# Second-layer gathers that wait for counted sums; the counts made once, in the first stage

## The reference

```python
# layer 2 (GIN): edge_attr is 100000 x 256
msg = relu(x[src] + edge_attr)
aggr = segment_sum(msg, dst)
h = relu((x + aggr) @ W1 + b1) @ W2 + b2
out = layernorm(x + relu(h), gamma, beta)
# layer 3 (GCN)
out = segment_sum((x @ W)[src] * edge_weight, dst) + b
```

## Time and profile before

| | |
|---|---|
| median of 3 runs | 6718.57 us (6707.67 to 6720.85) |
| profiled execution | 6709.51 us, span 6707.9 us |
| TensorE clock granted, mean over the span | 0.782 |
| stages in the trace (about) | first stage to 135 us; second layer's edges 1631 to 2834; third layer's edges 3038 to 4533 |

### The profile page before, as it was taken

The page is one execution under the profiler, slowest core; times in us unless marked ns, Lnnn a source line. Parts: engine busy times, 40 slices in busy tenths (PEclk is TensorE's granted clock), DMA queues, the critical chain, the costliest instruction groups (busy, mean ns, idle before and its releaser), DMA issues. The chain is left out here.

```text
span 6707.9 us, 101753 instructions
## 1 busy us (share of the span) xinstructions
PE 4589.8 (68%) x18270; PEld 3405.7 (51%) x18271; DVE 4578.5 (68%) x11385; ACT 2738.4 (41%) x8093; POOL 4024.3 (60%) x3678
## 2 busy tenths in 40 slices
PE   5466666650566666787777777766577777777799
PEld 4234434430333333476666666655455555555688
DVE  4466666676454454587777777766489989888554
ACT  0233333335333333252111111113298899888543
POOL 2666666633666666426888888881377777777110
PEclk8666676675767777897777777778788898988899
DMA  7344444424555655426888888886466666666110
GB/s 239 104 107 107 111 108 109 107 78 159 171 176 176 183 177 177 123 67 119 136 135 136 136 135 137 135 116 225 147 182 190 182 187 187 187 183 180 37 32 28
DMA packets 698838, 940.86 MB, mean 140 GB/s; under 512 B 99488, under 2 KB 555552, under 8 KB 698721
## 3 DMA queue, kind: packets, MB, share of 16 engines
q0 software_dynamic: 270624, 580.57, 37.7%
q1 hardware_dynamic: 408658, 339.19, 17.8%
q10 hardware_dynamic: 19440, 19.79, 0.9%
HBM read 756.06 MB, written 183.11 MB: 140 GB/s over the span
## 5 line engine op out<-in xcount | busy, mean ns | idle before, releaser
L1864 POOL DMA_INDIRECT gcn<-c_update,c_target x784 | 1227.4, 1566 | 265.0 <-issue 203.8
L696 POOL DMA_INDIRECT e_rows<-hrow,e_idx x832 | 820.7, 986 | 465.0 <-issue 234.8
L2240 POOL DMA_INDIRECT s_rows<-kv,s_idx x832 | 800.4, 962 | 397.1 <-issue 214.3
L1249 POOL DMA_INDIRECT g_rows<-x,g_idx x784 | 772.5, 985 | 388.1 <-issue 228.6
L759 PE MATMUL psum<-e_rows,e_onehot 128*128 128x265 f32 x1664 | 667.1, 556 | 292.5 <-DVE acc L853 124.3
L1368 PE MATMUL psum<-g_rows,g_onehot 128*128 x1664 | 606.0, 527 | 217.5 <-ACT g_rows L1272 169.9
L2354 PE MATMUL psum<-queries_sums,s_spread 128*128 x1664 | 523.7, 469 | 261.8 <-issue 153.4
L1330 DVE TENSOR_TENSOR acc<-acc,psum 128x1024 f32 x208 | 253.7, 1220 | 592.2 <-DMA n_bias<-in_l_bias 338.8
L759 PEld LDWEIGHTS psum<-e_rows,e_onehot 128*128 128x128 f32 x1664 | 396.9, 264 | 501.5 <-DVE acc L853 217.5
L1368 PEld LDWEIGHTS psum<-g_rows,g_onehot 128*128 128x128 f32 x1664 | 418.8, 264 | 421.9 <-issue 346.8
L1841 ACT COPY acc<-psum 128x512 f32<-128x512 f32 x208 | 121.9, 586 | 1157.2 <-PE psum L1795 618.9
(11 more groups left out here) (381 smaller groups left out, 9433.8 us busy)
## 6 DMA issues: line engine op xcount, KB each, us to landing
g_attr<-in_edge_attr SPq DMA_DIRECT2D x196, 512.0 KB
acc<-rows_src SPq DMA_DIRECT2D x208, 256.0 KB
e_drow<-rows_dloc SPq DMA_DIRECT2D x208, 128.0 KB
acc<-in_edge_feat SPq DMA_DIRECT2D x832, 32.0 KB
s_drow<-rows_dloc SPq DMA_DIRECT2D x208, 128.0 KB
n_sums<-gcn SPq DMA_DIRECT2D x100, 256.0 KB
e_rows<-hrow,e_idx POOLq DMA_INDIRECT x832
edge_rows<-c_edge_rows SPq DMA_DIRECT2D x208, 64.0 KB
```

The source lines that it names most:

```text
L696: pool.indirect_dma_start(rows[u][:, s, 0:D + H], None, k.hrow, bass.IndirectOffsetOnAxis(ap=idx[u][:, s:s + 1], axis=0)).then_inc(gathere ...
L1249: pool.indirect_dma_start(rows[:, s, :], None, k.x1, bass.IndirectOffsetOnAxis(ap=idx[:, s:s + 1], axis=0)).then_inc(gathered[n % ROUND], 16)
L1864: pool.indirect_dma_start(k.gcn[a], bass.IndirectOffsetOnAxis(ap=target[:, at:at + 1], axis=0), update[:, at, :], None, compute_op=ALU.add ...
L2240: pool.indirect_dma_start(rows[at.u][:, st, 0:2 * D], None, k.kv, bass.IndirectOffsetOnAxis(ap=idx[at.u][:, st:st + 1], axis=0)).then_inc( ...
```

## The change

The counts are made once, in `prepare`, and kept for both layers. `count_steps` is the old computation of the third layer (for each edge group the number of steps that start it or come before it); `count_groups` does the same over every fourth step, so it counts groups of steps. They are the ninth and tenth entries of `late_tables`. PE turns four columns into a row behind its last product of the loop, and DVE makes `k.steps_until` and `k.groups_until` of it.

In `gin_edges` for t = 1 to 8 POOL's wait for `summed` takes its value from `k.groups_until` at g-20, and the wait for `idx_ready` at a batch's first group is for 3 instead of 1, two copies of indices later. For t = 0 and t = 9 both stay. In `gcn_edges` the computation goes, and POOL reads `k.steps_until`; PE waits for `tables` in place of `done_ready`.

```diff
+            def count_steps():
+                for n in range(2):
+                    ch.tick(dve.tensor_scalar(limit[:, n:n + 1], k.lane[:], float(GROUP),
+                                              float(GROUP - 1 + n * GROUP * P), ALU.mult, ALU.add))
+                ch.wait()
+                for n in range(2):
+                    ch.then(dve.scalar_tensor_tensor(out=select[:, 0, :], in0=irow[:], scalar=limit[:, n:n + 1],
+                                                     in1=ones[:, 0:1].to_broadcast([P, STEPS]), op0=ALU.is_le,
+                                                     op1=ALU.mult, accum_out=until[:, n:n + 1]))
+
+            def count_groups():
+                starts = irow[:].rearrange("p (g s) -> p g s", s=GROUP)[:, :, 0]
+                for n in range(2):
+                    ch.then(dve.scalar_tensor_tensor(out=select[:, 0, 0:STEPS // GROUP], in0=starts,
+                                                     scalar=limit[:, n:n + 1],
+                                                     in1=ones[:, 0:1].to_broadcast([P, STEPS // GROUP]), op0=ALU.is_le,
+                                                     op1=ALU.mult, accum_out=until[:, 2 + n:3 + n]))
+                dve.sem_inc(until_ready, 1)
...
+            dve.wait_ge(until_turned, 1)
+            dve.tensor_scalar(k.steps_until[:], ps[0:1, 0, 0:2 * P], 2.0, 2.0, ALU.mult, ALU.add)
+            dve.tensor_scalar(k.groups_until[:], ps[0:1, 0, 2 * P:4 * P], 2.0, None, ALU.add)
...
+            pe.wait_ge(until_ready, 1)
+            for n in range(4):
+                ins = pe.matmul(ps[0:1, 0, n * P:(n + 1) * P], until[:, n:n + 1], k.ident[:], start=True, stop=True)
+            ins.then_inc(until_turned, 1)
...
                 g = t * (2 * ROUND) + n
+                exact = not isinstance(t, int)
                 if n % BATCH == 0:
-                    pool.wait_ge(idx_ready, t * BATCHES + n // BATCH + 1)
-                wait_if_any(pool, summed, g - 2 * ROUND + STALE + 1 + 2)
+                    pool.wait_ge(idx_ready, t * BATCHES + n // BATCH + (3 if exact else 1))
+                if exact:
+                    pool.wait_ge(summed, pool.value_load(k.groups_until[0:1, bass.ds(g - 2 * ROUND, 1)],
+                                                         min_val=1, max_val=GROUPS + 2))
+                else:
+                    wait_if_any(pool, summed, g - 2 * ROUND + STALE + 1 + 2)
...
             def make_tables():
                 ch = Chain(dve, tables)
-                ch.tick(dve.memset(one[:], 1.0))
...
-                for n in range(2):
-                    ch.tick(dve.tensor_scalar(limit[:, n:n + 1], k.lane[:], float(GROUP),
-                                              float(GROUP - 1 + n * GROUP * P), ALU.mult, ALU.add))
                 ch.wait()
-                for n in range(2):
-                    ch.then(dve.scalar_tensor_tensor(out=again, in0=irow, scalar=limit[:, n:n + 1],
-                                                     in1=one[:].to_broadcast([P, STEPS]), op0=ALU.is_le, op1=ALU.mult,
-                                                     accum_out=until[:, n:n + 1]))
-                dve.sem_inc(until_ready, 1)
...
-                dve.wait_ge(until_turned, 1)
-                dve.tensor_scalar(done_at[:], k.psum[0:1, TABLE_BANK + 2, 0:2 * P], 2.0, 2.0, ALU.mult, ALU.add
-                                  ).then_inc(done_ready, 1)
...
                 if isinstance(g, int) and g == 0:
-                    pe.wait_ge(until_ready, 1)
-                    for n in range(2):
-                        ins = pe.matmul(k.psum[0:1, TABLE_BANK + 2, n * P:(n + 1) * P], until[:, n:n + 1], k.ident[:],
-                                        start=True, stop=True)
-                    ins.then_inc(until_turned, 1)
-                    pe.wait_ge(done_ready, 1)
+                    pe.wait_ge(tables, 3)
...
-            pool.wait_ge(done_ready, 1)
             def scatter_pass(it, lap_at):
-                done = [pool.value_load(done_at[0:1, bass.ds(it * RING + q, 1)], min_val=GROUP, max_val=2 * STEPS + 2)
+                done = [pool.value_load(k.steps_until[0:1, bass.ds(it * RING + q, 1)], min_val=GROUP, max_val=2 * STEPS + 2)
```

More of the change, by code:

```diff
@@ L167, in allocate @@
     k.step_i = sb("step_i", [1, STEPS], I32)
+    k.steps_until, k.groups_until = (sb(f"{n}_until", [1, 2 * P], I32) for n in ("steps", "groups"))
     k.psum = ctx.enter_context(nc.psum_tensor("psum", [P, 8, 512], F32))
@@ L273, in prepare @@
         lane_is = sb("p_lane_is", [P, 2])
+        limit, until = sb("p_limit", [P, 2]), sb("p_until", [P, 4])
+        until_ready, until_turned = sem("p_until_ready"), sem("p_until_turned")
         pick = sb("p_pick", [P, 4, P])
@@ L515, in link_joints @@
                 dve.sem_inc(link_ready, 1)
-            late_tables = (mask_dlocs, mask_keys, find_stops, scale_gaps, scale_joints, scale_ends, link_back, link_joints)
+            def count_steps():
[15 more added lines that the diff above has]
+                dve.sem_inc(until_ready, 1)
+            late_tables = (mask_dlocs, mask_keys, find_stops, scale_gaps, scale_joints, scale_ends, link_back, link_joints,
+                           count_steps, count_groups)
             def take_pair(it, b):
@@ L1632, in gcn_edges @@
         slot_at = sb("c_slot_at", [1, STEPS], I32)
[L1633 to L1636, removed]
         we_sb = sb("c_we", [EDGE_D + 1, HEAD_D])
@@ L1649, in gcn_edges @@
         row_ready, row_spread, cleared = sem("c_row_ready"), sem("c_row_spread"), sem("c_cleared")
-        until_ready, until_turned, done_ready = sem("c_until_ready"), sem("c_until_turned"), sem("c_done_ready")
         block = ctx.enter_context(nc.Block())
@@ L1726, in make_tables @@
                     ch.tick(dve.tensor_copy(irow[:, n * HALF:(n + 1) * HALF], k.psum[:, TABLE_BANK + n, 0:HALF]))
-                for n in range(2):
-                    ch.tick(dve.tensor_scalar(limit[:, n:n + 1], k.lane[:], float(GROUP),
-                                              float(GROUP - 1 + n * GROUP * P), ALU.mult, ALU.add))
                 ch.wait()
-                for n in range(2):
-                    ch.then(dve.scalar_tensor_tensor(out=again, in0=irow, scalar=limit[:, n:n + 1],
-                                                     in1=one[:].to_broadcast([P, STEPS]), op0=ALU.is_le, op1=ALU.mult,
-                                                     accum_out=until[:, n:n + 1]))
-                dve.sem_inc(until_ready, 1)
                 ch.tick(dve.memset(again[:, 0:1], 0.0))
                 ch.then(dve.tensor_tensor(again[:, 1:STEPS], irow[:, 1:STEPS], irow[:, 0:STEPS - 1], ALU.is_equal))
-                dve.wait_ge(until_turned, 1)
-                dve.tensor_scalar(done_at[:], k.psum[0:1, TABLE_BANK + 2, 0:2 * P], 2.0, 2.0, ALU.mult, ALU.add
-                                  ).then_inc(done_ready, 1)
+                assert ch.n == 5
             def accumulate(it, q, slots):
```

## The result

The changed kernel takes 6881.04 us (median, 6875.23 to 6887.97) against 6718.48: a ratio of 1.0239, 95% interval 1.0227 to 1.0251; the medians lie 162.6 us apart. The forecast was 6752, slower, with a range up to 6870. The direction is right, the size is not, and the time lies 11 us above the range.

What follows compares the result with a forecast made beforehand. No compute engine alone was the limit: POOL's gathers and PE's late sums ran in lock step. 6709.5 + 45 (new gate, 32 batches) + 0.5 (first stage) - 2.8 (third layer) = 6752; range 6655 to 6870 for 8 in 10.

Steps and rivals of the forecast that it cites:

- faster rival: Second-layer gathers: the 2.8 us pause paid once for 5 groups, not 3 or 4; -42 us, 6665; chance 0.30.
- four cases: Loop batch under the new gate: 27.3, 29.8, 30.2 or 32.7 us; their average, 30.0, gave +45 us.
- untied cases: Two batch prices, 27.3 and 30.2 us, if the sum's increments aren't tied to POOL's last gather.
- run A: POOL's run in the old trace, 2738.30 to 2771.66: 33.4 us, read as 6 groups; five relus take 27.3.
- run B: POOL's run in the old trace, 1916.02 to 1943.80: 27.8 us, read as 5 groups; five relus take 30.2.
- Case B: The run B price if increments stay tied to POOL's last gather: moved by 2.5 us, 32.7 a batch.
- the base: Second-layer loop before the change: 916 us for 160 groups, 5.72 a group, 28.6 us a batch of 5.
- The rival "much slower": Second-layer gathers: sums stand still while POOL runs long, 35.5 us a batch, +221 us, 6930; chance 0.12.
- "no change" rival: Second-layer gathers: one limit replaces the other, 28.2 to 29.0 us a batch, for instance 6707 in total; chance 0.15.
- The signs: Expected profile, groups 20 to 179: one POOL stop a batch behind ACT's index copy, 3 to 7 us, some 150 in all.
- Third layer: With the counts gone, DVE gets free 2.9 us earlier before the first scatter: -2.8 us.
- First stage: Added counts: DVE's passes hidden, 0 (bounds 0 and 3.3); tensor_scalars at the stage's end 0.5 us (bounds 0 and 0.8).

## Why the prediction was right and wrong

**Right: the place, and the parts of the mechanism.** The sum waits of POOL went (127.1 us in the loop; 1.5 us are left in the whole view) and a stop behind the index copy took their place, 30 times. No add of the loop waits for its rows. Sums are held while POOL's run lasts, the second of the late ones until it is over, and the new gate stands further down the chain than the old one, as the prediction says against its faster rival: it put this at 3 us, and it is 5.7 us behind the let-go sum instead of 0.66.

**Wrong: the price of a batch, 30.0 us forecast, 34.1 measured.** The step that failed is the average over four cases at "The four average 30.0 us". Two of the four took the held increments as not tied to POOL's run, and one took run A, where the sum came in mid-run with 6.93 us of waiting. The case that applied was run B moved by 2.5 us, 32.7. The evidence for the tie stood in the prediction itself (POOL follows the sum by 0.66 us, 2.2 us after it had run dry), and the untied cases got half the weight without a row for them. Case B is short by 1.4 us. Run B had 19 gathers, not 20 (24.3 us from 1916.02 to the end of its last one, where the batch above has 25.2): 0.9 us. The let-go sum came 2.8 us after the run there and comes 3.2 us after it here: 0.4 us. From the relu to the gather are 2.6 us instead of 2.5.

**Wrong as well: the base, 28.6 us a batch.** The window of 916 us holds 623 gathers, not the 640 of 160 groups; a batch of the kernel before is 29.4 us. On this base 30.0 us would have been +19 us instead of +45. So this slip brought the forecast nearer to the result, which is luck. With the right base the measured batches give 32 x 4.7 = 150 us, and the groups 20 to 179 measured 146.

**The bounds.** The range's upper end came from 33.7 us a batch, under the 34.1 measured. The rival "much slower" has the nearest price with 35.5 us, but its reason (POOL runs long and nothing stops it) isn't enough: runs of 24 gathers cost 5.8 us a group. A and B had waits of 7 us and cost nothing extra because their gates opened with the let-go sum.

**The faster rival** fails on these chips. One pause for 5 groups is not 2.8 us but 8.9, since the gate stands 5.7 us behind the let-go sum. What spoke for it was misread: A has 23 gathers and B 19, so 33.4 and 27.8 us are 5.8 and 5.9 us a group, the same as the usual 23.3 for 4, and not 5.56. It is not right on the other kind of chip either, where the time is the same for both kernels. Nor does the "no change" rival hold where the forecast was scored, though on three chips it is what happens, for a reason it did not name: POOL is the limit there.

**The signs.** Stops of 3 to 7 us, some 150 us in all, were forecast; they are 8.3 to 9.2 us in the 29 even batches, and the view of the index copy counts 277.4 us. The releaser is named "issue" in the view of POOL.

**The small terms.** Value loads: 0, as said. Third layer: -2.9, forecast -2.8. First stage: +2.15, forecast 0.5, with bounds of 0 to 3.3 for the passes and 0 to 0.8 for the rest. The next pair's first copy comes at 101.91 instead of 99.83, and the loop doesn't win these 2.1 us back in the 0.9 us gaps that follow: the last operation starts at 131.95 instead of 129.22. Those gaps are waits for PE, so they were no cover for DVE's passes.

**What is not settled.** Shown: sums are held while POOL's gathers go out, longer in longer runs. Once the last gather of the kernel before is out, the last 18 sums start at most 0.5 us after their banks are closed. Shown too: bytes, attribute loads and the depth of the queue are not the reason. What ties PE's increments to POOL's gathers, whether the matmul or its increment is late, and why some chips do not have it, is open: the experiment that would have told the matmul from the increment came to a chip without holding. That the time follows the place of the gate at equal run length is read from runs of several kernels; no experiment moved the gate alone by a set time. The rule of the Trainium skill (SBUF — State Buffer, Who interferes with whom), that PE waits on no one, agrees with the trace on the chips near 6250 us. On the others it does not describe what DVE sees: there sums start up to 56 us behind PE's recorded closing. Whether PE itself waits there, no row shows.

## What to carry to other kernels

Before a wait is made rarer or moved, look at what it gates and at what has to happen between the event that ends the pause and the gate. Here POOL's pause ends with a held sum. A gate that opened with this sum cost 5.8 to 6.0 us a group at runs of 12 to 24 gathers; one that stood a relu, a copy and a load behind it cost 6.8, though it was asked only once in 5 groups. Count the instructions in the window that a price per batch is taken from: 623 gathers taken for 640 moved the base by 0.8 us. And where one semaphore is late in a way that nothing in the program explains, try the kernel on more than one chip before tuning around it.

## What the runs showed of the hardware

Chips differ by 7 to 8% on the same kernel. The kernel before takes 6718 to 6764 us on three or four of them (which chip the scored runs had is not on record) and 6249 to 6258 us on three others. On the first kind a sum that waits for an increment of PE started up to 56 us after PE's recorded closing while POOL issued indirect gathers without a stop, with TensorE at full and at half clock, and no less with half of the bytes. On the second kind the same program shows no such wait, and POOL issues the 784 gathers in 992 us instead of 1149. That is a third of the difference between the kinds; the first layer's 832 gathers take 1072 us instead of 1284 in the changed kernel, with 235 us of POOL's waits for PE down to 16.
